# A small GpSimd write behind every gather of the attention loop

## The reference

```python
qkv = (node_embeddings @ W_qkv).reshape(nV, N, 3 * H)       # 8 heads of 32
q, k, v = jnp.split(qkv, 3, axis=-1)
scores = jnp.einsum('phi,phi->ph', q[src], k[dst]) / jnp.sqrt(jnp.float32(H))
m = jax.ops.segment_max(scores, src, num_segments=nV)
e = jnp.exp(scores - m[src])
denom = jax.ops.segment_sum(e, src, num_segments=nV)
w = e / denom[src]
wv = w[:, :, None] * v[dst]
att = jax.ops.segment_sum(wv, src, num_segments=nV).reshape(nV, N * H)
pre = _layer_norm(att @ W_o + node_embeddings, ln1_g, ln1_b)
inter = jax.nn.gelu(pre @ W_i, approximate=False)
out = _layer_norm(inter @ W_out2 + pre, ln2_g, ln2_b)
```

## Time and profile before

| | |
|---|---|
| median of three runs | 6931.88 us |
| the profiled execution | 6926.02 us |
| its span, first to last instruction | 6924.2 us |
| granted TensorE clock, mean | 0.859 |
| the attention loop, first gather to last accumulate | about 4798 to 6436 us |
| in it: TensorE busy | 1286 of 1638 us |
| in it: VectorE busy | 1457 of 1638 us |
| in it: GpSimd busy | 879 of 1638 us (928 gathers) |
| in it: DMA engines busy, mean | 0.58 |

### The profile page before, as it was taken

One profiled execution on the slowest core, in us unless ns is written; L12 is line 12 of the kernel. 1 busy time (PEld: TensorE's weight loads), 2 busy tenths in 40 slices (PEclk: granted clock), 3 DMA queues, 4 the chain that ended last, 5 costly groups with the idle time before them and its releaser, 6 DMA issues.

```text
span 6924.2 us, 119002 instructions
## 1 busy us (share of the span) xinstructions
PE 5098.2 (74%) x23622; PEld 3740.3 (54%) x23625; DVE 5440.1 (79%) x13214; ACT 2578.1 (37%) x9112; POOL 4131.6 (60%) x6484
## 2 busy tenths in 40 slices
PE   7166676752777777796777777997777877777898
PEld 5044444431444444345666666885555555555687
DVE  8788777867877786557888887754999989888666
ACT  1032333321333333125555563112555555555111
POOL 0188888835888888367888883002555555555111
PEclk9586767766888888898999999997998889898899
DMA  4133333323444444335555554553555555556111
GB/s 125 32 100 94 101 101 102 101 83 108 123 121 129 126 127 124 99 122 172 159 156 153 163 150 136 162 161 112 164 159 160 162 157 159 153 156 155 54 44 36
DMA packets 449602, 865.25 MB, mean 125 GB/s; under 512 B 78488, under 2 KB 284424, under 8 KB 448906
## 3 DMA queue, kind: packets, MB, share of 16 engines
q0 software_dynamic: 194048, 574.45, 30.1%
q1 hardware_dynamic: 238442, 251.25, 11.6%
q10 hardware_dynamic: 16416, 31.99, 1.4%
HBM read 718.55 MB, written 298.46 MB: 147 GB/s over the span
## 4 chain that ended last, share of the span: by engine, by line
POOL 36%; PE 22%; DVE 19%; issue 9%; DMA 9%; POOLq 2%; ACT 1%; SPq 0%; DVEq 0%; ACTq 0%
POOL ring L755 17%; POOL big L1472 11%; PE ps L1598 5%; POOL pause L745 5%; DMA ring<-kv_d,gidx 3%; DMA ring<-xl_d,idx 3%; PE ps L2052 3%; PE ps L851 3%; PE ps L2069 3%; PE ps L1863 2%; POOLq L197 2%; DVE big L1956 2%; DVE big L1972 2%; DVE big L357 1%; DVE big L1981 1%
## 5 line engine op out<-in xcount | busy, mean ns | idle before, releaser
L851 PE MATMUL ps<-ring 128*128 x3528 | 1401.8, 529 | 781.1 <-SPq L768 514.8
L851 PEld LDWEIGHTS ps<-ring 128*128 128x128 f32 x3528 | 706.0, 245 | 1229.9 <-issue 1164.3
L825 ACT CAST ring<-ohb 128x128 f32<-128x128 bf16 x1764 | 524.2, 298 | 1682.2 <-DVE ohb L788 1645.3
L755 POOL DMA_INDIRECT ring<-xl_d,idx x832 | 849.5, 1021 | 469.2 <-DVEq L641 315.6
L1734 POOL DMA_INDIRECT ring<-kv_d,gidx x754 | 714.0, 947 | 588.1 <-issue 514.9
L1548 PE MATMUL ps<-big,ring 128*128 128x128 f32 x4928 | 777.4, 302 | 313.0 <-DVE big L1529 169.0
L755 POOL DMA_INDIRECT ring<-x_d,idx x832 | 838.2, 1007 | 136.6 <-issue 119.5
L1472 POOL DMA_INDIRECT big<-x_d,idx x832 | 810.4, 974 | 156.2 <-issue 134.1
L1548 PEld LDWEIGHTS ps<-big,ring 128*128 128x128 f32 x4928 | 661.6, 198 | 419.7 <-DVE big L1519 337.9
L885 POOL TENSOR_TENSOR lns<-lns,neg_half 128x1 f32<-128x1 f32 x294 | 181.8, 618 | 1050.9 <-DVE lns L880 1050.9
L798 DVE TENSOR_TENSOR big<-big,ps 128x257 f32 (+1 forms) x1764 | 752.4, 427 | 61.9 <-issue 31.8
(11 more groups left out here) (414 smaller groups left out, 9488.0 us busy)
## 6 DMA issues: line engine op xcount, KB each, us to landing
bas_d<-big SPq DMA_DIRECT2D x1232, 128.0 KB
att_d<-wreg SPq DMA_DIRECT2D x464, 132.0 KB
big<-bas_d SPq DMA_DIRECT2D x49, 1024.0 KB, 5.5
x_d<-ring SPq DMA_DIRECT2D x147, 128.0 KB, 1.7
gh_d<-aside ACTq DMA_DIRECT2D x49, 384.0 KB
ring<-xl_d,idx POOLq DMA_INDIRECT x832
ring<-x_d,idx POOLq DMA_INDIRECT x832
big<-x_d,idx POOLq DMA_INDIRECT x832
```

The lines of the kernel that those rows point to most:

```text
L755: nc.gpsimd.indirect_dma_start(out=rows[:, j, :], out_offset=None, in_=table, in_offset=bass.IndirectOffsetOnAxis(ap=idx_of(c), axis=0)).t ...
L851: T.matmul(ps[k][:, 0:D], ohf[:, k, :], rows[:, slot, :].rearrange("p a d -> p (a d)"), start=True, stop=True)
```

## The change

One line is added to the attention gather loop: behind each gather, GpSimd writes zeros into the first four columns of the tile `pause` (which nothing reads), and waits until this write has completed. The sequence object `q` is handed in for it.

```diff
-        def att_gather_pool(pool):
+        def att_gather_pool(pool, q):
             def step(c, j, i):
...
                 nc.gpsimd.indirect_dma_start(
                     out=rows3(j, 1).rearrange("p s f -> p (s f)"), out_offset=None, in_=kv_d,
                     in_offset=bass.IndirectOffsetOnAxis(ap=gidx[:, g, j % GRP:j % GRP + 1], axis=0)).then_inc(got3[g][0], 16)
+                q.link(nc.gpsimd.memset(pause[:, 0, 0:4], 0.0))
             walk(pool, N3, R3, 0, step, flat=True)
...
-            att_gather_pool(pool)
+            att_gather_pool(pool, q)
```

## The result

The changed kernel takes 6947.81 us (median of 15 runs), the kernel before 6931.88 us (median of 15 as well). The ratio is 1.0034, with a 95% interval from 1.0026 to 1.0043: the change costs 24 us (18 to 30). The two medians alone lie 16 us apart and the two means 22, so the cost is known to a few us and not to one. Forecast were 42 us; the direction was right, the size too large. The profiled execution of the changed kernel took 6943.67 us, 17.7 us more than that of the kernel before.

A forecast was written before the change was run, and what follows sets the result against it. VectorE was taken to set the attention loop's pace, held up a little by gathers. Terms 18 + 21 + 5 - 2 = 42 us made the median 6974 us; own range 6954 to 6994, wider range 6941 to 7005.

The forecast's parts named there:

- The latency behind the write: At a group's second to fourth gather: start 0.29 us after the write, period 1.36 us, 0.11 more than before.
- bounds of 0.06 and 0.80 by rows 6 and 7: Wait inside groups: between linked-instruction and group-start latencies, two gathers starting earlier layers (0.36, at least 0.22 us) gave 0.29.
- The rival in which the full latency stands behind every write: Attention loop: each gather takes 1.83 to 1.87 us, GpSimd becomes the bound, +184 us, 7116; chance 0.09.
- the filled gap: Inside groups the wait hides in existing idle time, leaving only group-start terms of 9 us, 6941 or less; chance 0.11.
- the shorter handover: Inside groups a gather follows the write after 0.06 us, period 1.13 us; -15 us, 6917; chance 0.04.
- the prediction's own two rules: A group's first gather starts 0.80 us after its slots' release, or 0.30 us behind the gather before, if later.
- The start behind the group before: Where GpSimd is late, a group's first gather starts 0.92 us behind its predecessor's end, not 0.30.
- the second term: Group 0's later start behind group 3: 27 batches lose 0.67 us, 10 lose 0.31, 19 nothing; 21 us.
- Group 0's own spacing: Inside group 0, three periods each longer by 0.11, 0.33 us a batch over 56 batches; 18 us.
- a way to be wrong: Stated failure case: idle time 0.29 but VectorE waits no longer, since transfers land sooner when spaced out; no size given.
- Group 3: Where VectorE waits for group 3's gathers, 15 times, each costs 0.33 us; 5 us.
- What is given back ... about -2 us: In 16 batches VectorE did not wait for group 0, so some tenths of slack are used up first; about -2 us.

The follow-up runs named there:

- e8: Kernel before, without the write: at a group's start the slot wait is placed last and the semaphore increment left out; 6904.51 us, ratio 0.9967.
- e5: Changed kernel, but with write and wait behind only the first three gathers of each group; ratio 1.0022 to the kernel before.
- e7: Changed kernel, but with four linked writes behind each of group 0's first three gathers and none elsewhere; ratio 1.0134 to the kernel before.
- e6: Changed kernel, but with write and wait behind only the fourth gather of each group; ratio 1.0021 to the kernel before.
- e1: Changed kernel, but GpSimd waits for the write before the last one, not the newest; ratio 1.0013 to the kernel before, on the 7997.49 us chip.
- e4: Changed kernel, but with write and wait behind only the gathers of groups 1 and 2; ratio 1.0010 to the kernel before, on the 7997.49 us chip.

## Why the prediction was right in direction and too large

**The latency behind the write (0.29 us, a period of 1.36).** Measured 0.27 and 1.34. The choice between bounds of 0.06 and 0.80 by rows 6 and 7 held, and e8 shows why: the short latency belongs to a wait inside the gather. The rule of the Trainium skill that was weighed there (Perfetto Trace Analysis, section "DMA Instruction — SWDGE (GPSIMD)": decoded and queued before its semaphores are looked at) agrees with the gathers of 520 floats as well, 0.27 us in the changed kernel and 0.26 to 0.28 in e8. The rival in which the full latency stands behind every write is dead, and so are the filled gap and the shorter handover. (That rival was given "all 232 group starts" in its favour; of the 224 that reuse slots, 171 start 0.80 us after their release, and 51 stand 0.30 to 0.32 us behind their predecessor, as the prediction's own two rules say.)

**The start behind the group before (0.92 us).** Measured 0.96. Where slots are late, the start was taken as unchanged at 0.80 us behind L1972; it is 0.90 to 0.91 now. In plain batches group 0 starts 0.71 us later (2.57 to 3.28). Over 37 such batches this is 26 us, where the second term had 21. In stretched batches VectorE has waited for TensorE before it releases the slots, GpSimd stands ready by then, and group 0 starts only 0.09 us later (2.58 to 2.67): the second term rightly charged these batches nothing.

**Group 0's own spacing (18 us).** 0.30 us in plain batches, about as forecast (0.33). But VectorE goes on with the rows of the last gather 0.14 us sooner after its start. The same is seen in e5 (0.19 us for 0.23 of spacing) and in e7 (0.52 for 1.67), and in the batches alone in which VectorE waits for these rows: 4.10 us before, 3.90 in the changed kernel, 3.93 in e5, 3.54 in e7. So here a gather lands faster when the one before it is further away. The prediction had named this as a way to be wrong and not counted it. It is some 6 us over all batches.

**Group 3 (5 us).** Its waits grew from 8.5 to 10.9 us, 2.4 us.

**The term that was mis-sized: "What is given back ... about -2 us", with "the other wait times of VectorE don't depend on gathers".** A plain batch became 0.72 us longer (27.03 to 27.75), where the two terms on group 0 charge 0.33 us and, on average, some 0.6. A stretched batch became 0.07 us longer (29.55 to 29.62), where 0.33 was charged. At the mix of the kernel before this makes 37 x 0.72 + 18 x 0.07 = 28 us, give or take 6, which agrees with the measured 18 to 30. The parts at the same mix, measured against forecast: the start of group 0 28 us for 21, its spacing 13 for 18, group 3 2 for 5, sooner rows -6 for nothing. These make 37 us, and the batches became only 28 longer, so that another 9 or 10 us came back. All in all some -16 us stand where the prediction has -2. Of the 9 or 10, the waits of VectorE for TensorE in plain batches, which fell from 0.18 to 0.07 us a batch, are 4 us: there TensorE seems to catch up while VectorE waits for rows. The rest is no larger than the error of such a sum, and I can't assign it. In particular it is not shown that stretched batches swallow a delay inside the group: those of e5 became 0.18 us longer for 0.27 of spacing, and those of e7 1.09 us for 1.67, as much as plain ones. So the mechanism and its places were right. The size was too large: 6947.81 us lies below the forecast's own range of 6954 to 6994, and inside the wider one, from 6941, only because that one was drawn out for the filled gap, a mechanism that did not occur.

**The profile of one execution.** Its 55 batches took 18.5 us more. With 28 from the two kinds, the rest is that it had 5 stretched batches fewer, at 1.9 us each. The time that a profile shows for this loop moves with that number, so a comparison of two profiles as totals would have been off by a third here.

**What stays open.** Whether the number of stretched batches belongs to the chip, the execution or the kernel. In the same order, the measured times less those worked out at the old mix are -4 us (changed, 13 stretched), +14 (e5, 24), +1 (e6, 27), +33 (e7, 31) and +16 (e8, 31). The large ones go with the number, as if it were partly the kernel's own, but e6 doesn't, and the kernel before was profiled once only, not beside e5 to e8; a second profile of it wasn't made. The granted clocks of all executions on that chip bear on it too: 0.862 on average for the kernel before (24 executions), 0.861 for e5, 0.863 for e6, 0.859 for e7 and 0.858 for e8. So e7 and e8 had a lower clock over all their executions, not in the profiled one alone, and e5 had not. For e5, whose cost is all in that number, this means that its 15 us are measured and not explained. Nor was the write without the wait (e1), or the change in groups 1 and 2 alone (e4), tried on a chip on which gathers count, so that a small cost of the write itself is not excluded; nor was a wait for slots taken pair by pair, which e8 suggests as the next step.

## What to carry to other kernels

Put the wait that is met last into the expensive instruction itself, with no semaphore instruction between the two: what stands behind a semaphore instruction has its preparation still before it when the wait ends. Here that alone is worth 0.5 us at each group start whose slots come late, and 0.33% of the kernel. Price a delay by the path from the release of a buffer to its use, batch by batch, and ask for each batch which of the two comes last at every start. Where the release came late anyway, a delay of the issuing engine costs little (0.09 us for 0.71 here); a delay behind the release costs there as much as elsewhere. Before comparing two profiles as totals, sort the batches by their other waits and by the granted clock.

## What was not expected of the hardware

- A gather behind a separate semaphore instruction starts 0.80 us after its release (0.90 in the changed kernel, where two stand there), one whose wait is its own 0.26 to 0.28 us after it, with the same 128 rows of 2080 bytes.
- Of four gathers 1.25 us apart the last is followed by its rows 4.02 us after its start, 3.50 us when they are 1.81 us apart.
- One chip ran the same kernel in 7997 us, which took 6927 to 6932 us elsewhere. The profiles taken there, of e1 to e4, have idle times of several us on VectorE (up to 5.5 in e1) that nothing on the core explains, and a change that costs 0.22% elsewhere gained 0.29% there.
- The lower clock costs by where it falls. A batch of 16 chunks takes 27.0 us, and 29.6 when TensorE is granted 0.50 to 0.55 of its clock between the third and the fifth pair.
